# A two-layer change inside a fused transformer stack: the 16-head attentions go from whole steps to half steps

## The reference, cut to what matters

```
L2 attention (head width 8):            L2 feed-forward begins with (head width 4):
att  = q @ k.T / sqrt(8)                scores = rope(q) @ rope(k).T / sqrt(4)
mask = tril(ones, k=-1)                 scores = where(tril, scores, -inf)
att  = softmax(att * mask)              attn   = softmax(scores)
out  = (att @ v) @ Wr + br              x      = x + (attn @ v) @ w_up   (then a mixture of experts)
```

## Time and profile before

| | |
|---|---|
| median of 3 runs | 5070.35 us (5070.07 to 5073.6) |
| the profiled execution, its own time | 5074.89 us |
| span of that execution, first to last instruction | 5073.3 us |
| mean granted TensorE clock | 0.793 of 2.4 GHz |
| busy: PE, VectorE, ScalarE, GpSimd | 72%, 55%, 28%, 14% |

### The profile page before, as it was taken

How to read it: one execution, slowest core, us unless ns; L and a number is a source line. 1 busy time by engine, 2 the same in 40 slices (tenths; PEclk the granted TensorE clock), 3 DMA queues, 4 the chain that set the end, 5 groups by cost and what they waited for, 6 DMA issues and landing times. The chain is left out here.

```text
span 5073.3 us, 75445 instructions
## 1 busy us (share of the span) xinstructions
PE 3648.2 (72%) x29138; PEld 2466.5 (49%) x29138; DVE 2782.0 (55%) x7164; ACT 1420.9 (28%) x2783; POOL 724.8 (14%) x464
## 2 busy tenths in 40 slices
PE   1558877886455788788746678778874577887885
PEld 1536554454353565455435456544553455554454
DVE  3575644546657454445665745444565674544456
ACT  1223423321313332332131333223203033332320
POOL 1122300000113230000011322000001142200000
PEclk9569878898657898888755789879875588887897
DMA  0000000000000000000000000000000000000000
GB/s 24 1 18 18 1 1 2 2 26 1 10 1 18 19 1 1 2 2 26 1 10 1 18 18 1 2 2 6 21 1 10 0 18 18 1 2 2 11 16 5
DMA packets 54906, 42.61 MB, mean 8 GB/s; under 512 B 14419, under 2 KB 51206, under 8 KB 54534
## 3 DMA queue, kind: packets, MB, share of 16 engines
q1 hardware_dynamic: 54534, 37.62, 2.5%
HBM read 34.97 MB, written 2.10 MB: 7 GB/s over the span
## 5 line engine op out<-in xcount | busy, mean ns | idle before, releaser
L167 POOL TENSOR_TENSOR ln_rstd<-ln_var_eps,neghalf 128x4 f32<-128x4 f32 x128 | 129.7, 1014 | 2201.0 <-DVE ln_var_eps L179 2200.7
L1957 DVE TENSOR_REDUCE l2r_m<-l2r_bank_ring 128x1 f32<-128x384 f32 (+3 forms) x352 | 207.2, 637 | 255.8 <-PE l2r_bank_ring L1806 255.8
L1957 DVE TENSOR_REDUCE l2a_m<-l2a_bank_ring 128x1 f32<-128x384 f32 (+3 forms) x352 | 207.2, 637 | 246.0 <-PE l2a_bank_ring L1806 246.0
L1188 POOL TENSOR_TENSOR l1t_ss<-l1t_ss,neghalf 128x16 f32<-128x16 f32 x64 | 240.4, 3756 | 464.5 <-DVE l1t_ss L1243 464.5
L2071 ACT ACTIVATE l2r_P<-l2r_bank_score 128x512 f32<-128x512 f32 x320 | 168.6, 594 | 287.1 <-PE l2r_bank_score L1833 159.0
L2071 ACT ACTIVATE l2a_P<-l2a_bank_score 128x512 f32<-128x512 f32 x320 | 169.2, 597 | 265.9 <-PE l2a_bank_score L1833 138.6
L1432 PE MATMUL l1t_ring<-l1f_qkv,x_normT 128*128 128x512 f32 x384 | 229.4, 749 | 13.1 <-ACT x_normT L1097 13.1
L1516 PE MATMUL l1t_score<-l1t_q_head,l1t_k 128*128 128x256 f32 (+1 forms) x896 | 207.1, 363 | 0.0
L1797 PE MATMUL l2r_bank_ring<-l2r_k_head,l2r_q_head 32*128 32x256 f32 (+3 forms) x1024 | 181.2, 530 | 33.0 <-DVE l2r_m L1957 26.4
L1797 PE MATMUL l2a_bank_ring<-l2a_k_head,l2a_q_head 32*128 32x256 f32 (+3 forms) x1024 | 175.4, 512 | 26.2 <-DVE l2a_m L1957 22.1
L1397 ACT ACTIVATE l1t_P<-l1t_score 128x512 f32<-128x512 f32 x176 | 105.2, 598 | 225.1 <-PE l1t_score L1516 224.9
(11 more groups left out here) (555 smaller groups left out, 8488.6 us busy)
## 6 DMA issues: line engine op xcount, KB each, us to landing
l2e_w<-in_L_ffn_w SPq DMA_DIRECT2D x96, 128.0 KB, 2.3
l1f_qkv<-in_L_ffn_wqkv SPq DMA_DIRECT2D x8, 768.0 KB, 4.3
l1f_tables<-in_l_tables SPq DMA_DIRECT2D x8, 512.0 KB, 5.4
l1f_w<-in_L_ffn_w SPq DMA_DIRECT2D x8, 341.0 KB
x_res<-in_L_attn_hidden_states SPq DMA_DIRECT2D x8, 256.0 KB, 3.3
l1f_wo<-in_L_ffn_wo SPq DMA_DIRECT2D x8, 256.0 KB, 4.6
l2a_q_head<-l2a_shiftT SPq DMA_DIRECT2D x128, 2.0 KB
l2r_q_head<-l2r_shiftT SPq DMA_DIRECT2D x128, 2.0 KB
```

Of the source, the lines that this page charges most:

```text
L167: pool.tensor_tensor(b.rs[:, p, :], b.ve[:, p, :], b.neghalf[:, 0:NT], ALU.pow).then_inc(s["post_rstd"] if post else s["pre_rstd"], 1)
L1188: pool.tensor_tensor(ss[:, n % 2], ss[:, n % 2], b.neghalf[:, 0:2 * H8], ALU.pow).then_inc(s["rn_ready"], 1)
L1957: dve.tensor_reduce(self.m[:, n, 4 * g + u:4 * g + u + hb], bank, AX, ALU.max).then_inc(s["max_ready"], 1)
```

## The change

The 20 steps become 40 half steps. An even half has the scores of row groups 0 and 1, an odd one of row groups 2 and 3 (`groups`). Units are dealt out in the order of row groups 2, 3, 0, 1, and up to two of them are woven between the four rounds of score matmuls of a half; the others follow. Values of a half come two halves later (`PV_LAG` = 2).

The masks of units with one head (j = 2, 3) leave TensorE: VectorE reads the bank together with a wide mask row and takes the maximum in one `tensor_tensor_reduce`, whose elementwise result goes to a scratch in bf16. The score masks leave TensorE too: GpSimd zeroes the masked part of the exponentials with `affine_select` (`pool_masks`, 4 per tile). The shift of a tile is turned in half `end`, the tokens and outputs of a tile one and three halves after its last values. The projection of 7 of the 8 tiles and l2a's post-norm of the first sequence move ahead of the last tile's end; the bias matmuls become one of 512 columns for each sequence. The preparation is reordered: first maxima ahead of the values' projection of the second sequence, shift 1 before the steps, and in l2r own banks for both sequences' rotations.

```diff
+        self.halves = 2 * len(self.steps)
+        self.units = [[(g, u) for u in range(0, 4, self.PER_BANK[j]) for g in (2, 3, 0, 1)] for j, _ in self.tiles]
...
+        begin = 0
         for n in range(2, len(self.tiles)):
-            at = range(self.first[n - 1] - 1, self.first[n] - 1)
+            end = max(begin + 2, 2 * self.first[n] - 3)
             for i in range(len(self.units[n])):
-                self.max_at[at[i * len(at) // len(self.units[n])]].append((n, i))
+                self.max_at[begin + i * (end - begin) // len(self.units[n])].append((n, i))
+            self.turn_at[end].append(("shift", n, "shiftT_ready"))
+            begin = end
+        for n in range(len(self.tiles)):
+            last = 2 * self.first[n + 1] - 1 + self.PV_LAG
+            self.turn_at[last + 1].append(("token", n, self.token_read))
+            self.turn_at[last + 3].append(("oT", n, "oT_ready"))
...
+    def groups(self, h):
+        return (0, 1) if h % 2 == 0 else (2, 3)
...
+    def pe_half(self, pe, h):
+        units = self.max_at[h]
+        hb = self.PER_BANK[self.tiles[units[0][0]][0]] if units else 1
+        if hb > 1:
+            views = [self.max_view(pe, *unit) for unit in units[:2]]
+            for u in range(4):
+                for unit, view in zip(units[:2], views):
+                    if u * hb % 4 == 0:
+                        self.pe_max_piece(pe, *unit, view, u * hb // 4)
+                self.pe_scores(pe, h, u)
+            self.pe_max_mask(pe, units[:2], views)
+            views = [self.max_view(pe, *unit) for unit in units[2:]]
...
         for u in range(4):
+            if u % 2 == 0 and u // 2 < len(units):
+                self.pe_max_piece(pe, *units[u // 2], self.max_view(pe, *units[u // 2]), 0)
+            self.pe_scores(pe, h, u)
+        for unit in units[2:]:
+            self.pe_max_piece(pe, *unit, self.max_view(pe, *unit), 0)
...
+        for h in range(len(self.turn_at)):
+            if h < self.halves:
+                self.pe_half(pe, h)
+            if 0 <= h - self.PV_LAG < self.halves:
+                self.pe_values(pe, h - self.PV_LAG)
+            if h == self.halves:
+                project(pe, 0, 0, NT)
+                project(pe, 1, 0, NT - 1)
+            for kind, n, _ in self.turn_at[h]:
+                turn[kind](pe, n)
+        project(pe, 1, NT - 1, NT)
...
+    def pool_masks(self, pool):
+        for n in range(len(self.tiles)):
+            k = self.first[n + 1] - 1
+            for g in range(4):
+                pool.wait_ge(s["p_ready"], 4 * k + g + 1)
+                P = self.P[:, (4 * k + g) % self.P_RING]
+                pool.affine_select(out=P, in_=P, compare_op=ALU.is_gt if self.strict else ALU.is_ge, fill=0.0, base=0,
+                                   pattern=[[0, 4], [1, 128]], channel_multiplier=-1).then_inc(s["p_masked"], 1)
...
-            dve.tensor_reduce(self.m[:, n, 4 * g + u:4 * g + u + hb], bank, AX, ALU.max).then_inc(s["max_ready"], 1)
+            if hb == 1:
+                use = self.m_first[n] + i
+                dve.wait_ge(s["max_ready"], use - 3)
+                ins = dve.tensor_tensor_reduce(self.masked[:, use % 4, 0:N], bank[:, 0, :], self.wide[:, S - N:], 1.0, MASKED,
+                                               ALU.add, ALU.max, into)
+            else:
+                ins = dve.tensor_reduce(into, bank, AX, ALU.max)
```

More of the change, by code:

```diff
@@ L1749, in place_max, with first_units, ended @@
             self.place("max", (n, i), "max_ready", self.m_first[n] + i + 1)
[L1751 to L1765, removed]
-        if k + 1 < len(self.steps) and k + 1 in self.first:
-            due.append(("shift", self.first.index(k + 1), "shiftT_ready"))
-        for kind, sem, lag in (("token", self.token_read, 2), ("oT", "oT_ready", 3)):
-            n = self.last_step(k - lag)
-            if n is not None:
-                due.append((kind, n, sem))
-        return due
+    def first_units(self, n, start, stop):
+        return [(n, i) for i in range(start, stop)]
+    def groups(self, h):
+        return (0, 1) if h % 2 == 0 else (2, 3)
+    def ended(self, h):
+        h -= self.PV_LAG
+        return self.steps[h // 2][0] if h > 0 and h % 2 and (h + 1) // 2 in self.first else None
     def claim(self, pe, kind, n):
@@ L1813, in pe_scores, with pe_first_max @@
+    def pe_first_max(self, pe, n, start, stop):
+        units = self.first_units(n, start, stop)
+        views = [self.max_view(pe, *unit) for unit in units]
+        for c in range(4):
+            for (n, i), view in zip(units, views):
+                self.pe_max_piece(pe, n, i, view, c)
+        self.pe_max_mask(pe, units, views)
+    def pe_scores(self, pe, h, u):
+        s, (n, kt) = self.s, self.steps[h // 2]
         j, p = self.tiles[n]
         keys, queries = slice(kt * 128, (kt + 1) * 128), slice(j * 128, (j + 1) * 128)
-        if kt == 0:
+        if kt == 0 and h % 2 == 0 and u == 0:
@@ L1827, in pe_score_mask @@
-    def pe_score_mask(self, pe, k):
-        n, kt = self.steps[k]
-        if kt < self.tiles[n][0]:
-            return
-        neg = self.b.neg["col_gt" if self.strict else "col_ge"]
-        for g in range(4):
-            pe.matmul(self.s_bank[g][:, :], self.b.ident_bf[:], neg[:].unsqueeze(1).to_broadcast([128, 4, 128]),
-                      start=False, stop=True, skip_group_check=True).then_inc(self.s["s_ready"], 1)
-    def pe_values(self, pe, k):
-        s, (n, kt) = self.s, self.steps[k]
+        for i, g in enumerate(self.groups(h)):
+            if u == 0 and h >= 2:
+                pe.wait_ge(s["p_ready"], 2 * (h - 2) + i + 1)
+            rows = slice(32 * g, 32 * g + 32)
+            ins = pe.matmul(self.s_bank[g][:, u * 128:(u + 1) * 128], self.k[rows, p, u, keys],
+                            self.q[rows, p, u, queries], start=u == 0, stop=True, skip_group_check=True)
+            if u == 3:
+                ins.then_inc(s["s_ready"], 1)
@@ L2269, in _ @@
                 step(dve.tensor_tensor(xn, xn, at.y[p][:, :], ALU.add))
+            keep(0)
+            at.dve_finish(dve, step, len(at.tiles) - 1)
+            keep(1)
             step.settle()
```

344 lines of the change are left out of this document (175 added, 169 removed).

## The result

The changed kernel takes 5155.44 us (median of 4, 5143.11 to 5160.4) against 5071.81 (5070.07 to 5073.6) in the same session: ratio 1.0161, 95% interval 1.0143 to 1.018. The forecast was 4910, range 4850 to 5015: wrong in sign and outside the range. The profiled execution took 5160.4, with a span of 5158.7.

A forecast was written before the change was run, and what follows sets the result against it. TensorE and its waits were taken to bound the steps. Gains of 11.4 + 15.1 + 3.5 + 0.7 + 9.7 + 1.7 = 42.1 us an iteration, 168 in four, gave 4902, forecast as 4910 for small waits; range 4850 to 5015.

The forecast's parts named there:

- a busy row group holds up its own queue and not the others': TensorE in the steps: matmuls for free row groups pass those waiting; a half of tile 7 then takes 2.5 us.
- the layout: Steps laid out by stretches of halves at full clock: 111.6 us to l2a's last o, 110.3 in l2r.
- first rival: TensorE keeps program order, so free groups' scores wait: steps 123.8 us instead of 111.6, total about 5005; chance 0.10.
- 5.5 us an attention were kept for stretches at 1.2 GHz: Steps: 5.5 of the earlier kernel's 8.2 us, mostly slow-clock stretches, were kept on top of the full-clock times.
- third rival: TensorE falls to 1.2 GHz in the steps: about 5470 if throughout, sign turning at 30% of their time; chance 0.06.
- Unit prices: TensorE times from one step: 0.87 streaming, 0.21 change of rows, eight values 0.57; a half without a unit 1.65 us.
- VectorE's instruction: New masking maximum on VectorE: 0.78 us for 512 keys, 0.65 for 384, staying under TensorE.
- second rival: VectorE's maximum costs the scan's rate, 1.225 us, and bounds halves 5 to 20: total about 5015; chance 0.10.
- GpSimd's mask: Score masks moved to GpSimd: 0.61 us for 512 columns, hidden on diagonal steps.
- End of l2a: From the last o to the next part: 7.2 us instead of 16.94, a gain of 9.7.
- Preparation: Stage before the steps: a gain of 3.5 us in l2a and 0.7 in l2r.
- Fourth rival: Half steps bring nothing, only ends and preparation gain, 62 us: total about 5008; chance 0.08.

The follow-up runs named there:

- fit_early: Changed kernel, with the units of tiles 2 to 4 alone dealt to halves whose scores are in the other two row groups; 5055.77 us, ratio 0.997.
- filler: Changed kernel plus four 128-row, 512-column matmuls in each of halves 2 to 5, whose result the scores write over; 5014.55 us, ratio 0.988.
- order_only: Changed kernel, only issue order altered in halves 21 to 28: second group's unit, first's scores, first's unit, second's scores; 5083.69 us, ratio 1.0028.
- unit_fit: Changed kernel with the fitting deal: each unit, but one of tile 3, in a half whose scores use the other two row groups; 4810.42 us.
- unit_last: Changed kernel, same deal, with the units issued behind the half's scores instead of between them; 5546.61 us, ratio 1.0889.
- fit_pe_masks: unit_fit with the score masks back on TensorE and none on GpSimd; 4844.96 us, ratio 0.9555.
- whole_steps: Changed kernel with whole steps instead of half steps; masks, preparation and ends as changed; 4912.32 us, ratio 0.9683.

## Why the prediction was wrong

A gain of 42.1 us an iteration was forecast, and the first iteration lost 24.0: l2a's steps were forecast 33.7 us too short and l2r's 37.0, and the gain elsewhere 4.5 too small. Over all four iterations the loss is 85.4 us by the two spans, 21.4 each.

**The step that failed first**: "a busy row group holds up its own queue and not the others'". The windows of the earlier trace rows could not show it. In them each row group's matmul comes in its turn, and starts together are what either rule gives. At full clock, halves 0 to 38 take 113.7 us (19.4, 13.3, 16.9, 18.7, 27.2, 18.2: halves 0 to 4 from fit_early's second l2a, the others from filler's) where the layout had 103.8. The 19.4 belongs to the fitting deal and is too low for the changed kernel's, which no run has at full clock there; at 0.50 in l2r the two deals take 31.7 and 35.1 us, so an estimate is 1.7 more, 115.4 in all. In the layout halves 0 to 8 were right or up to 1.7 too long and 29 to 38 right within 0.4; 9 to 20 were 5.0 too short and 21 to 28 6.3. In those, one-head units stand in the scores' row groups. With half 39 and what follows (9.2 at full clock, in fit_early) the steps come to 122.9 to 124.6 us; the first rival's layout, 123.8 and 2.2 for the projection, was right within some 3, and the forecast's, 113.8, 9 to 11 too short. The Trainium skill ("TensorE: Matmul & The Clock Gate", Part 2) says that matmuls stay in program order and only weight loads are pulled ahead. The runs agree with it in the main: order_only is 5.9 us a stretch faster by order alone. They differ in one point: by the records one score started ahead of an earlier one that waited (826.19).

**The larger term**: 5.5 us an attention were kept for stretches at 1.2 GHz, and 27 to 28 came in l2a (142.1 less 115.4 or 113.7), more in l2r, whose halves 0 to 4 run at 0.50. Of the 33.7 us that l2a's steps miss, order is thus 9 to 11 and the clock 23 to 25. The third rival had 0.06 for "in my layout PE streams some three quarters of the time, as today". That took time under way for the measure; the profile has it at 1.00 in the stretch that stayed at 1.2 GHz. By its own rule (the sign turns where 30% of the steps' time falls) it was the case: a mean clock of 0.78 is 44%. It was also wrong to give rivals 1 and 3 chances as if they excluded each other. Serial row groups keep few rows at work, and in the early halves the clock goes with them: halves 5 to 8 run at 0.50 in all eight passes of the changed kernel, and at 0.93 to 1.00 in all eight of unit_fit. filler, which leaves the order as it is and brings most of the clock back, comes out at 5014.55, and the first rival said 5005; this is luck in part, since filler also pays for its own matmuls and for halves 0 to 4 still at 0.51 to 0.87. unit_last had rival 3 almost whole: 5546.61 for 5470.

**Point by point.**
- Unit prices: right. A half without a unit takes 1.64 us (1.65), a half with two row groups back to back 2.50 (2.52).
- VectorE's instruction: a mean record of 0.691 for 512 and 0.556 for 384 keys, and a second record of 0.083 that reads the accumulator. The second does not add to the first: it lies under the end of the first, the next instruction starts at the same moment (808.17), and from start to start it is 0.61 us for 512 keys, not the 0.78 forecast. The reduction before was at 0.60, and not 0.63 (817.73 in the earlier trace rows: three in 1.89 us, the last of 0.69). The second rival is out. The Trainium skill ("VectorE: DVE Perf Modes", Two Vector instructions with no wait between them) says that an instruction which also writes its accumulator is two, and the trace has two; the 0.86 that the prediction worked out from that, with the shift's 0.17 behind, is out.
- GpSimd's mask: 0.634 (0.61); TensorE waits for it 11.1 us in all four l2a passes, in 16 places.
- Masks off TensorE: 6.7 us an attention for the score masks (fit_pe_masks), at full clock. Halved steps pay 102 us against whole ones (unit_fit 4810.42, whole_steps 4912.32), but only with the units in the other row groups, and little of it is gained at equal clock. Of 18.4 us in the first l2a's steps (122.7 and 104.3), 3.2 lie in halves 16 to 29 (33.1 and 29.9, both at 1.00), nothing behind them, and 15.2 ahead of them, where whole_steps runs at 0.81 and unit_fit at 1.00.
- The wait for the DMA: 50.8 us to 6.1. The wait for VectorE's maxima: 54.5 to 34.8 (29.6, and 5.2 for the one-head units).
- End of l2a 6.6 us behind the last o (7.2), of l2r 2.0 (2.1). From the first score of half 39 to the last o 10.8, or 9.2 at full clock, where 10.1 were forecast.
- Preparation gained 6.7 and 1.3 for 3.5 and 0.7. l2a's is at a clock of 0.77 and not 0.69, which may be the rest; no run tests it.
- Fourth rival (half steps bring nothing): at full clock this is about the case. Halves 15 to 28 take 45.9 us, and the seven steps 8 to 14 took 43.8 before, with the same units, both at 1.00. The loss in the total is the clock's.

Open: why the clock comes back in some l2r passes of order_only and not in others, why one l2a pass of unit_fit and all its l2r passes begin below the full clock with the fitting deal, and why fit_early's spread is 72 us. That these are passes at the border between the two levels is argued, not shown.

## What to carry to other kernels

Matmuls on parts of the rows run side by side only if the program's order lets them: when one waits for a busy row group, one more for a free group still starts, and what follows that stands, for the free groups too. Deal the work so that neighbours in the program use different row groups (here 345 us between two deals of the same matmuls), or issue one group's whole run before the next group's first.

A TensorE that is always busy can still be at half clock. Read the granted clock by stage, and ask how much of the array works at once; a change that thins it must be costed at both levels. Compare two kernels on a stretch where both have the same clock before you put a difference down to the program. Evidence for a queue's rule must come from a window in which the two rules differ.

## What the runs showed of the hardware

- At a granted clock of 0.50, with a matmul under way 51.02 of 51.02 us (halves 21 to 28 of fit_early's third l2r), TensorE stayed there while scores and units worked in one or two groups of 32 rows, beside value matmuls of 128 rows and 5 columns (9 in l2a). Four 128-row matmuls of 512 columns in each of four halves had it at 1.00 from half 5 to half 28 in all eight passes, and 32-row ones in none.
- The same halves held either level once entered (21 to 28: 27.23 us at 1.00, 51.02 at 0.50, in one execution of fit_early). Ten executions of that kernel lie within 1.4%, the fastest with a mean clock of 0.791 and the slowest with 0.778.
- A masking maximum on VectorE (two operands, PSUM and SBUF, written in bf16) comes every 0.61 us back to back for 512 keys, a plain reduction every 0.60. The record of 0.083 that reads the accumulator lies under the end of the first and the start of the next.
